# Two transformer layers, eight batches: the next batch's first-layer routing moved into the second layer's experts, its scatters to the front of the attention run

## What is computed

```python
xn = _layernorm(x)
x = x + _L0_attn_ref(xn, ...) + _L0_ffn_ref(xn, ...)      # first layer: 8 heads, top-2 of 8 experts
xn = _layernorm(x)
x = x + _L1_attn_ref(xn, ...) + _L1_ffn_ref(xn, ...)      # second layer: linear attention, top-4 of 8

def _L0_ffn_ref(hidden_states, router_w, w_gate, w_up, w_down):
    logits = x @ router_w.T
    routing_weights, selected = sparsemixer_eval(logits, 0.01)   # the two best experts of a token
    ...
        h = jax.nn.silu(x @ w_gate[e].T) * (x @ w_up[e].T)
        out = out + dense_w[:, e:e + 1] * (h @ w_down[e].T)
```

## Time and profile before

| | us |
|---|---|
| median of 3 runs | 2558.47 |
| lowest and highest | 2558.06, 2561.96 |
| the profiled execution, its own time | 2557.68 |
| its span, first to last instruction | 2555.9 |
| PE busy | 2315.6 (91%) |
| DVE busy | 1982.7 (78%) |
| ACT busy | 1660.5 (65%) |
| POOL busy | 737.2 (29%) |
| mean granted clock of PE | 0.962 |

### The profile page before, as it was taken

The page is one execution under the profiler, slowest core; times in us unless marked ns, Lnnn a source line. Parts: engine busy times, 40 slices in busy tenths (PEclk is TensorE's granted clock), DMA queues, the critical chain, the costliest instruction groups (busy, mean ns, idle before and its releaser), DMA issues.

```text
span 2555.9 us, 64898 instructions
## 1 busy us (share of the span) xinstructions
PE 2315.6 (91%) x25503; PEld 1656.1 (65%) x25503; DVE 1982.7 (78%) x3435; ACT 1660.5 (65%) x3050; POOL 737.2 (29%) x621
## 2 busy tenths in 40 slices
PE   6989989899898998989989899898998989988998
PEld 3667566665666666766667666676666766666665
DVE  6778877788778887787876878868778687786986
ACT  4866558665686656775567755767457684585845
POOL 2220432205322052221522215212253023530234
PEclk8999999999999999999989999999999999999999
DMA  7110211103111121111211112111121112211022
GB/s 250 51 42 2 106 54 43 42 19 104 39 45 39 43 84 35 47 38 43 88 32 49 34 47 88 33 48 30 63 76 34 44 30 76 68 35 49 19 78 63
DMA packets 99124, 141.35 MB, mean 55 GB/s; under 512 B 11523, under 2 KB 60620, under 8 KB 98316
## 3 DMA queue, kind: packets, MB, share of 16 engines
q1 hardware_dynamic: 90636, 120.41, 14.9%
q0 software_dynamic: 8192, 16.79, 2.3%
HBM read 101.84 MB, written 31.13 MB: 52 GB/s over the span
## 4 chain that ended last, share of the span: by engine, by line
PE 60%; DVE 20%; issue 10%; ACT 8%; POOL 1%; SPq 0%; DVEq 0%; DMA 0%; ACTq 0%; POOLq 0%
PE ps L1552 11%; PE ps L1723 7%; DVE neg_max L1209 7%; PE ps L1745 6%; PE ps L1760 6%; PE ps L1559 6%; PE ps L1634 5%; ACT probs L821 4%; PE ps L1656 3%; PE ps L1509 2%; DVE ffn L1352 2%; PE ps L1573 2%; DVE probsT L1219 2%; DVE key_low L977 2%; PE ps L1645 1%
## 5 line engine op out<-in xcount | busy, mean ns | idle before, releaser
L1209 DVE TENSOR_REDUCE neg_max<-ps 128x1 f32<-128x1024 f32 x512 | 622.2, 1216 | 85.9 <-PE ps L1723 79.3
L821 ACT ACTIVATE probs<-ps,neg_max 128x1024 f32<-128x1024 f32 x512 | 577.0, 1127 | 76.1 <-DVE neg_max L1209 72.8
L1552 PE MATMUL ps<-shared,w_split 128*128 128x512 f32 x1536 | 471.1, 443 | 18.2 <-ACT ffn L872 11.6
L1745 PEld LDWEIGHTS ps<-ident,probs 64*128 64x128 f32 x8192 | 338.4, 145 | 172.3 <-issue 134.7
L706 POOL TENSOR_TENSOR probs<-ffn,shared 128x512 f32<-128x512 f32 x208 | 287.7, 1383 | 410.6 <-DVE ffn L1352 183.4
L1745 PE MATMUL ps<-ident,probs 64*128 64x64 f32 x8192 | 364.7, 231 | 41.4 <-issue 28.5
L1552 PEld LDWEIGHTS ps<-shared,w_split 128*128 128x128 f32 x1536 | 288.9, 193 | 165.0 <-issue 62.9
L872 ACT ACTIVATE ffn<-ps,room_of_gate 128x512 f32<-128x512 f32 x256 | 175.0, 683 | 270.5 <-PE ps L1552 270.5
L1723 PE MATMUL ps<-shared,query_a 64*128 64x512 f32 x1024 | 268.6, 521 | 84.5 <-ACT probs L821 62.2
L1760 PE MATMUL ps<-probsT,latent 128*32 128x128 f32 x8192 | 327.0, 279 | 12.9 <-DVE o_latent L1202 12.7
L805 ACT COPY probsT<-ps 128x512 f32<-128x512 f32 x512 | 303.2, 592 | 25.8 <-PE ps L1745 24.3
(11 more groups left out here) (231 smaller groups left out, 3501.7 us busy)
## 6 DMA issues: line engine op xcount, KB each, us to landing
w_split<-w_parts SPq DMA_DIRECT2D x132, 256.0 KB, 2.6
shared<-gate_rows SPq DMA_DIRECT2D x64, 512.0 KB, 4.4
y_rows<-probs SPq DMA_DIRECT2D x40, 256.0 KB, 2.2
x_in<-in_x SPq DMA_DIRECT2D x9, 512.0 KB, 4.1
out<-x_mid SPq DMA_DIRECT2D x8, 512.0 KB, 3.2
ffn<-in_gate_up SPq DMA_DIRECT2D x1, 2048.0 KB, 8.7
probsT<-in_gate_up SPq DMA_DIRECT2D x1, 2048.0 KB, 13.4
w_down<-in_down SPq DMA_DIRECT2D x2, 1024.0 KB
```

Source lines behind the costliest of these rows:

```text
L821: nc.scalar.activation(probs[:, t % 3, :], banks(2 * (t % 2)), ACT.Exp, bias=neg_max[:, t % 4:t % 4 + 1], accum_out=row_sum[:, g % 2, t % ...
L1209: nc.vector.tensor_reduce(neg_max[:, t % 4:t % 4 + 1], banks(2 * (t % 2)), X, ALU.max, negate=True).then_inc(max_ready.sem, 1)
L1552: mm = nc.tensor.matmul(ps[:, bank, :], w_split[:, f % CHUNK_SLOTS, h, k * P:(k + 1) * P], tokens[:, half], start=(part == 0), stop=(part ...
L1745: mm = nc.tensor.transpose(ps[:, turn_bank(t, c), k * HQ:(k + 1) * HQ], probs[rows, t % 3, k * P:(k + 1) * P], ident[rows, rows])
```

## The change

Six things change; the numbers of a line are those of the printed kernel before.

- From the second batch on, the routing is made in the second experts of the batch before: `route_two` and `places` are advanced by units of `NEXT_ROUTE` and `NEXT_PLACES`, and PE's prefix products stand at the end of unit 20. The pair tensors lie in `probs` there and not in `ffn`. The products of unit 22 wait for `prefix_taken`, because both use bank 7.
- In the first batch all stays in run 0. Everywhere the two pair operations of POOL move to DVE (`ranks`).
- On POOL the 16 scatters come first in a batch and the addition of `b_o` (L674) after them; on SP the load of `xs` comes before that of `x_in`.
- `both_on_act` holds for one tile in eight in both runs.
- `tokens(0)` (PE), `tokens_high(0)` (ACT) and `tokens_low(0)` (DVE) move two steps forward: from behind step 34 to behind step 33, ahead of step 34, into bank 1 and not bank 2.
- `chosen_experts` waits for the run's last copies only at its first transposes of results.

```diff
+TOKENS_STEP = QUAD_STEPS + T_LAG - 2
+NEXT_ROUTE = {10: 2, 17: 2, 18: 3, 20: 2, 22: 2}
+NEXT_PREFIX = 20
+NEXT_PLACES = {20: 1, 23: 4, 24: 3, 25: 3, 27: 4}
...
 def both_on_act(t):
-    run, i = divmod(t, NT * QUAD)
-    return i % 2 == 0 if run == 0 else i % 8 == 3
+    return t % 8 == 3
...
+                sp.wait_ge(scattered.sem, scattered.at(b, 16 * 2 * NT))
+                sp.sem_inc(rows_complete.sem, 1)
+                if index > 0:
+                    sp.wait_ge(down_done.sem, down_done.at(b, 0))
+                sp.dma_start(xs, x_rows[:, :].rearrange("(j p) d -> p j d", p=P)).then_inc(xs_loaded.sem, 16)
...
-                pool.wait_ge(pos_ready.sem, pos_ready.at(b, 1))
+                pool.wait_ge(pos_ready.sem, pos_ready.at(b, 0))
...
-                    if 0 < w < PLACES_STEP - 1 or PLACES_STEP + PLACES_STEPS <= w < QUAD_STEPS + 1:
+                    if index == 0 and 0 < w < PLACES_STEP - 1:
 
                         next(route, None)
...
                 for w in range(QUAD_STEPS + T_LAG):
                     attention_step(w)
+                    if w == TOKENS_STEP:
+                        tokens_low(0)
...
+                    if index + 1 < BATCH:
+                        if u == min(NEXT_ROUTE):
+                            dve.wait_ge(down_done.sem, down_done.at(b, 1))
+                            dve.wait_ge(rows_stored.sem, rows_stored.at(b, 16))
+                        for _ in range(NEXT_ROUTE.get(u, 0)):
+                            next(next_route, None)
+                        for _ in range(NEXT_PLACES.get(u, 0)):
+                            next(next_place, None)
...
-                    if g == 0 and i == NT // 2 - 1:
...
+                    if index == 0 and g == 0 and i == NT // 2 - 1:
+                        prefixes(None)
...
+                        if index + 1 < BATCH:
+                            pe.wait_ge(prefix_taken.sem, prefix_taken.at(b, 1))
...
+                    if u == NEXT_PREFIX and index + 1 < BATCH:
+                        prefixes(b)
```

More of the change, by code:

```diff
@@ L258, in two_layer_kernel @@
         gate_wT = probs[0:E, 1, :]
+        next_pairs = [probs[:, 1, i * BANK:(i + 1) * BANK].rearrange("p (n e j) -> p n e j", n=NT, e=E) for i in range(2)]
+        next_room = probs[:, 1, 0:BLOCKS * E].rearrange("p (j e) -> p j e", e=E)
         gate_bc = shared[:, 2 * SEQ:(2 + GATE_SLOTS) * SEQ].bitcast(F32).rearrange("p (s c) -> p s c", s=GATE_SLOTS)
@@ L828, in attention_step @@
                         copy_xT(b, 0, 0, 2)
-                for w in range(QUAD_STEPS + T_LAG):
-                    attention_step(w)
                 def tokens_high(q):
@@ L1042, in _, with ranks @@
             for index in range(BATCH):
-                b, count[0] = Sequence(index), 0
+                b = Sequence(index)
                 def wide(v):
                     return v.unsqueeze(2).to_broadcast([P, NT, E])
-                def ranks(logits):
+                def ranks(logits, pairs):
+                    pair_a, pair_b = pairs
                     by_j = logits[:, :, :].unsqueeze(2).to_broadcast([P, NT, E, E])
@@ L1167, in route_four @@
                     yield
-                    yield from ranks(logits)
+                    yield from ranks(logits, (pair_a, pair_b))
                     dve.wait_ge(r_exp_done.sem, r_exp_done.at(b, 3))
@@ L1184, in experts_add @@
                             ps[:, 6 + c, :].rearrange("p (n d) -> p n d", d=D), ALU.add).then_inc(y_added.sem, 1)
[L1187 removed]
+                route, place = route_two(None, (pair_a, pair_b)), places(None, 7, cmp_room)
+                next_route, next_place = route_two(b, next_pairs), places(b, 7, next_room)
+                weights = route_weights()
                 def split_low():
@@ L1288, in outputs @@
                                           ps[:, 5 + q % 2, 0:len(part) * D]).then_inc(ys_ready.sem, 1)
-                assert next(route, "end") == "end" and next(place, "end") == "end"
+                assert index > 0 or next(route, "end") == "end" and next(place, "end") == "end"
                 for j in range(BLOCKS + BLOCK_DOWN_LAG + 1):
@@ L1459, in _ @@
                         queries_rest(u - NEXT_KEYS)
+                    if index + 1 < BATCH:
[6 more added lines that the diff above has]
+                            next(next_place, None)
                 if index + 1 < BATCH:
+                    assert next(next_route, "end") == "end" and next(next_place, "end") == "end"
                     for h in range(QUAD):
@@ L1465, in _ @@
                     experts_add(b)
-                assert count[0] == DVE_STEPS, count[0]
         @block.tensor
@@ L1611, in experts, with tokens, prefixes @@
                         mm.then_inc(y_mm.sem, 1)
-            def chosen_experts(b, beside):
-                def tokens(q):
-                    if q == 0:
-                        pe.wait_ge(xs_loaded.sem, xs_loaded.at(b, 16))
-                    else:
-                        pe.wait_ge(xs_low_ready.sem, xs_low_ready.at(b, q))
-                    for i, j in enumerate(group_blocks(q)):
-                        mm = nc.tensor.transpose(ps[:, 2, i * P:(i + 1) * P], xs[:, j, :], ident[:, :])
-                    mm.then_inc(xsT_mm.sem, 1)
+            def tokens(b, q):
+                if q == 0:
+                    pe.wait_ge(xs_loaded.sem, xs_loaded.at(b, 16))
+                else:
+                    pe.wait_ge(xs_low_ready.sem, xs_low_ready.at(b, q))
+                for i, j in enumerate(group_blocks(q)):
+                    mm = nc.tensor.transpose(ps[:, token_bank(q), i * P:(i + 1) * P], xs[:, j, :], ident[:, :])
+                mm.then_inc(xsT_mm.sem, 1)
+            def prefixes(made):
+                pe.wait_ge(chosen_ready.sem, chosen_ready.at(made, 1))
+                counts = 2 * P + (NT + 1) * E
+                nc.tensor.matmul(ps[:, 7, 2 * P:counts], before[:, :],
+                                 chosen[:, :, :].rearrange("p n e -> p (n e)"), start=True, stop=False)
+                for m in range(NT):
+                    mm = nc.tensor.matmul(ps[:, 7, 2 * P + (m + 1) * E:counts], ones,
+                                          chosen[:, m, :].unsqueeze(1).to_broadcast([P, NT - m, E]),
+                                          start=False, stop=(m == NT - 1))
+                mm.then_inc(prefix_mm.sem, 1)
+            def chosen_experts(b, beside):
                 def gate_up(j):
@@ L1829, in _ @@
                     attention_step(w)
+                    if w == TOKENS_STEP:
+                        tokens(b, 0)
                 pe.wait_ge(exp_done.sem, exp_done.at(b, NT * QUAD))
```

120 lines of the change are left out of this document (47 added, 73 removed).

## The result

The changed kernel takes **2590.07 us** (median of 4 runs, 2584.71 to 2593.66), the kernel before, in the same comparison, 2559.54 (2558.06 to 2561.96): 1.0118 times as long, 95% interval 1.0104 to 1.0131. The profiled execution has a span of 2588.1 us at a mean granted clock of 0.952; before it was 2555.9 at 0.962. All times given here are of executions in the faster of the two states that a program has on this chip (one execution of the kernel before, beside experiments 1 to 3, took 3133.9 us at a mean clock of 0.65 and isn't counted). The direction was as forecast. The size was not: +30.5 us where +8.5 was forecast, outside the range.

The account below looks back on a forecast made before the run. No engine bounds all stages: PE and ACT in run 0, PE in the second experts around unit 20. Per batch 6.45 + 2.0 - 7.45 = +1.0 us, times seven, plus +1 for the first batch: 2567 us, range 2545 to 2583.

Parts of the forecast that it names:

- The wait for `chosen`: At unit 20, PE waits ahead of the prefix products for DVE's chosen pairs: 4.35 us a batch.
- the later end (951.4): Late time for `chosen`, if a POOL instruction gets in between DVE's two comparisons: 0.5 us more a batch.
- the middle value: Time taken for `chosen` on DVE, 950.9, between 950.4 and 951.4.
- The moved prefix: Prefix products moved from run 0 to the end of unit 20 add 2.1 us of PE work there.
- The clock behind the wait: After the prefix wait PE's clock falls to 1.2 GHz, losing 2.0 us a batch (0 to 3.4).
- Run 0: Gain of 7.45 us a batch (5.9 to 8.3): opening and prefix 2.9, five groups 2.9, end 1.65.
- The first batch: Keeps its routing in run 0, with more work on DVE: about +1 us (-1 to +3).
- The pieces of unit 10: Small routing pieces on DVE in unit 10, claimed to hide in idle time at no cost.
- the clock holds: Rival 2: the clock stays at 1.00 behind the prefix wait; batch -1.0 us, kernel 2553; chance 0.16.
- no wait: Rival 3: `chosen` is ready before PE's prefix; a batch wins 5.3 us, kernel 2522; chance 0.09.
- Rival 5: More lost behind the wait: `chosen` at 951.4, clock loss 2.95, unit 23 partly uncovered; 2577 to 2583 us; chance 0.15.
- the halves win nothing: Rival 4: run 0's groups stay at 7.83 us; batch +3.9 us, kernel 2587; chance 0.07.

Follow-up runs that it names:

- experiment 1: Changed kernel with the next batch's pair operations (comparisons, multiplication, addition, rank) moved into DVE's gaps beside units 15 to 17: 2537.9 us.
- experiment 2: Changed kernel with unused PE products of 512 columns ahead of the prefix at unit 20: 2568.3 us with five, 2577.7 us with two.
- experiment 6: Kernel of experiment 1 with five unused products once in the first batch's opening, shifting all behind them: 2540.5 us.
- after with the old split: Changed kernel with run 0's halves split as in the kernel before, every other tile's high half on ACT: 2616.5 us.
- experiment 3: Run 0's split of halves swapped: changed kernel with the old split, 2616.5 us; kernel before with the new split alone, 2558.0 us.

## Why the prediction was wrong in size

1. *The wait for `chosen`*: forecast 4.35, measured 4.08 in the batch shown, 4.0 in the mean. Right within 0.4. POOL got in between the comparisons, as the later end (951.4) assumed, and yet `chosen` came nearer to the middle value. That the wait is the cause is shown by experiment 1.
2. *The moved prefix*: forecast 2.1, measured 2.37 at the full clock (the stretch of experiment 1 less that of before). Right within 0.3. Together with the wait that is 6.4, and the forecast had 6.45.
3. ***The clock behind the wait*: this step failed.** I took 2.0 us a batch, by the 5.9 us of slow clock in the opening of run 1 and with a part of it falling in the wait. Experiment 2 gives 3.67 to 3.95. The stretch of run 1 was no measure for this place. The clock fell at most 0.9 us before the wait ended, so nearly nothing of the slow time lay in the wait, and in five of seven batches it was 10.2 us long. And nearly all of it met work bound by PE. Against the same rows at the full clock in experiment 2, the batch shown loses 1.9 us on the prefix, 1.7 on unit 21 (3.63 from its start to the next unit's, instead of 1.95) and 0.9 on unit 22, 4.5 together. The error is 1.7 to 2.0 us a batch, 12 to 14 us in all, of the 22 that were missed. The Trainium skill's rule that I weighed ("TensorE: Matmul & The Clock Gate", section "HAM oscillation — how this bites in real kernels"), a loss of half the slow time, comes nearer than my value here: it gives 5.1 for 10.2 us and 3.4 for 6.8 us, and the stretch from beta lost 4.4 and 3.0 to the clock. But it needs the length, and that had been taken from another place.
4. *Run 0*: 7.45 forecast, 7.30 measured, though divided otherwise. The opening gave 3.89 and not 2.9; 0.7 of that is because I had compared it in a batch where it was short (17.96; the mean was 18.70). Groups and end gave 3.41 and not 4.55: the groups are 7.33, since DVE with 30.35 of 32 us and PE with 31.73 are now full as well, and the end gave 1.05 and not 1.65.
5. *The first batch*: +1 forecast (-1 to +3), +2.1 measured.
6. ***The pieces of unit 10*: this step failed too.** The prediction let "the other pieces, in units 10 and 20 to 27" hide, by a row of idle time at 957.38, which stands behind unit 20. From unit 10 to the key base DVE has next to no idle time. The two pieces came through to PE as 0.8 us of longer wait ahead of beta in each of the seven batches: 5.5 of the 8.9 us that the stretch from the first experts to beta grew in the profiled execution. The seven batches stand against the eighth, and nothing else of the routing lies between its two ends. No run moved these two pieces, so that they cost the 5.5 us is read from the traces and not tested. The other 3.4 us of the 8.9 are open: slow clock that falls differently on the second experts (63.3 to 68.5 us for the same work in experiment 6) fits them but isn't shown. One kernel (after with the old split) has 193.43 in this stretch, half way between before and after.
7. *The rivals*: "the clock holds" and "no wait" didn't happen in this kernel. Experiment 2 made the first happen (2568.3 with its unused products, where the prediction had 2553), experiment 1 the second (2537.9, where it had 2522). Rival 5 was the one nearest to what happened, by its second part (the full loss of clock), and its 2.95 was still too small. That the halves win nothing was refuted by experiment 3.

## What to carry to other kernels

Work put on one engine ahead of a point where the bounding engine needs its result costs the wait, and then nearly as much again by the clock, if what follows is bound by TensorE: here 4.0 and 3.7 to 3.95 us. So look in the trace for DVE's gaps upstream of that point before choosing the step; the same five instructions in the gaps turned +31 us into -22. Look for the gaps at the very unit where a piece is put: a piece of 64 columns in a full stretch of DVE still made TensorE wait eight units later. Read such a term in every batch, not in one, and read the slow clock's length at places where a wait of that size meets that kind of work.

## What the runs showed of the hardware

- A wait of 4.0 us let the clock fall to 1.2 GHz for 6.8 or 10.2 us, in seven batches of seven. With 1.7 us of products in it, it held in two batches of seven and fell for 3.4 us in four, with the same idle time of 2.20 us before in all six, and for 6.8 us in one, after 1.96; with 4.3 us of products it held in all.
- One product of 0.86 us in a pause of 0.86, just ahead of sixteen small products of the router, gave 17 us over eight batches (0.7% of the kernel). The mean clock rose from 0.961 to 0.976. In the kernel before, it gave 6 us; there the opening of run 0 ran slow for nearly 14 us in four batches of seven instead of one.
- More clock isn't always time: 0.976 to 0.989 was worth nothing that the medians could show (2520.6 and 2519.9).
- A comparison of 512 columns on DVE took 0.68 us alone and 1.78 beside a POOL instruction of 1.68; a subtraction of 64 columns took 1.26 beside one of 1.27.
